# Layer 1's tail keys: future exponentials zeroed by GpSimd after the exponential, instead of a constant-mask matmul before it

## The chip, the cores and the metric

One Trainium2 chip, one of its cores. The metric is the device time of one execution in microseconds (us); the median of the runs is compared. The engines are TensorE (PE, with its weight loads as PEld), VectorE (DVE), ScalarE (ACT), GpSimd (POOL) and SyncE (SP), which issues most transfers.

## The reference, cut to what matters

Two layers of gated cross attention with a feed-forward part, on x of 4 batches x 512 rows x 128 channels; the keys and values come from a context of 154 rows per batch; 16 heads of 8 channels. What the change touches is layer 1's attention:

```python
scores = einsum('bhtd,bhsd->bhts', q, k) / sqrt(8)
causal = triu(full((512, 154), -inf), k=1)      # key s is seen by query t only if s <= t
attn = softmax(scores + causal, axis=-1)
out = einsum('bhts,bhsd->bhtd', attn, v)
x = x + tanh(g_xattn[1]) * (out @ Wo.T + bo)
```

Layer 0's attention has no causal mask. The feed-forward part of layer 1 is a recurrence over the 4 batches, with a gate of three matmul pairs for each.

## The kernel before, in words

Everything stays in SBUF. Each attention layer runs over the 4 batches as a software pipeline. For each batch there are 20 score tiles (index t, one per slot). Tiles 0 to 15 hold one head each: 128 keys on the partitions, 512 queries in a row. Keys 128 to 153 don't fit, so they are packed: tiles 16 to 19, the *tail tiles*, hold four heads each, in four blocks of 32 partitions; row r of a block is key 122 + r (TAIL0 is 122, OWN is 6, so rows 6 to 31 are the keys from 128 on). In layer 1 queries 0 to 127 see none of these keys, so a tail tile has only 384 queries.

For a tile, TensorE makes the scores in one of two PSUM banks (`scores`, L975 for the 16 main tiles, L981 for the tail tiles), ScalarE writes the exponential into the ring sb_pr of 8 tiles (`exps`, L766), and TensorE multiplies four tiles at a time with the values (`weigh`, L1007): rounds 0 to 3 take the main tiles, and two more calls, *tail0* and *tail1*, take the four tail tiles together. Both tail calls need the last exponential of the batch (tile 19). The sums go to two PSUM banks, which VectorE transposes and divides (L1332 to L1345); TensorE applies the output weights (L1016), VectorE adds the residual (L1351), and POOL and VectorE normalise.

Since only two score banks exist, the scores of tile k wait for the exponential of tile k - 2. The order of each engine's work is written out by hand: PE_PLAN, ACT_PLAN and DVE_PLAN give a slot (0 to 19) to each piece, and POOL's order is a loop over i. In iteration i the score tiles of batch i run, beside the tail calls of batch i - 1 (slots 1 and 3), the output product of batch i - 1 (slot 8), and the search for each query's largest score for batch i + 1 (L947, with its own mask L951, reduced by VectorE at L1312). Iteration i = 4 of layer 1 has no score tiles; there the tail calls of batch 3 come straight behind the last tile of iteration 3. The gate matmuls of the recurrence (`state` L1027 and `step` L1033, each run as two passes) are placed in the slots of iterations 3 and 4; `keep` and `renew` (L1366, L1373, L1376) update its state on VectorE.

The causal mask of layer 1 is made in two ways before the change. For the main tiles POOL zeroes the exponentials after ScalarE wrote them: `past(b, r)` (L614), one affine selection over four tiles, 128 partitions x 4 x 128, four times a batch; `weigh` waits for its semaphore past_r. For the tail tiles TensorE adds a constant of -2^126 to the scores before the exponential, with a second matmul of the identity by 32 columns of constants (L984, `maskE`), once for each tail tile:

```python
ins = pe.matmul(ps[:, q0:T], KT[:, b, t - H, :], Q4[n % 3][:, t - H, q0:T],
                start=True, stop=(layer == 0), skip_group_check=True)
if layer == 1:
    ins = pe.matmul(ps[:, P:P + 32], identr[:, :], maskE, start=False, stop=True, skip_group_check=True)
```

Only 32 of the 384 queries (128 to 159) can lie before one of these keys, so the mask has 32 columns.

POOL's loop in iteration i of layer 1: `past(i, 0)` to `past(i, 2)`, the normalisation of batch i - 1 (`normed`, L620 to L637), `past(i, 3)`, and `biased` for batch i + 1 (L598).

Of the kernel before, what the change touches and what calls it, by code (L numbers as in the profile page):

```python
# [8 lines left out]
F32R = mybir.dt.float32r  # L9
I16 = mybir.dt.int16  # L10
U16 = mybir.dt.uint16
ALU = mybir.AluOpType
# [3 lines left out]
P = 128  # L16
B, T, C = 4, 512, 128
TT = T // P
S = 154
H, D = 16, 8  # L20
G, J = 4, 4
NF = 3
TAIL0 = S - 32
OWN = P - TAIL0
SCALE = float(D) ** -0.5
EPS = 1e-5
NEG = -2.0 ** 126
# [9 lines left out]
TILES = H + G  # L37
# [3 lines left out]
PRING = 8  # L41
# [158 lines left out]
def program(nc, x, w, wkr, ctxT, tailT, wffn, cols, rows, consts, masks, out):  # L200
    with ExitStack() as ctx:  # L201
        def sb(name, shape, dt=F32):
            return ctx.enter_context(nc.sbuf_tensor("sb_" + name, shape, dt))

        def bank(name):
            return ctx.enter_context(nc.psum_tensor("ps_" + name, [P, 512], F32))

        def sem(name):
            return ctx.enter_context(nc.semaphore(name))
# [18 lines left out]
        ident = consts_sb[:, 0:P]  # L228
        own = consts_sb[:, P:P + 1]
        lowrow = consts_sb[:, P + 1:P + 2]  # L230
        cmask = sb("cmask", [P, 2 * P + 32])
        identr = sb("identr", [P, P], F32R)
        maskr = sb("maskr", [P, 2 * P + 32], F32R)
        maskM, maskT, maskE = maskr[:, 0:P], maskr[:, P:2 * P], maskr[:, 2 * P:2 * P + 32]
        ones = sb("ones", [P, P])
        onesr = sb("onesr", [2, P], F32R)
        bhl = sb("bhl", [2, 2, C], F32R)
# [26 lines left out]
        with ExitStack() as stretch:  # L264
            def sb_here(name, shape, dt=F32):
                return stretch.enter_context(nc.sbuf_tensor("sb_" + name, shape, dt))
# [16 lines left out]
            pr = sb_here("pr", [P, PRING, T])  # L283
# [27 lines left out]
        top = [bank(f"top{n}") for n in range(MRING)]  # L311
# [32 lines left out]
        nmh_r, nms_r, nmT_r = sem("nmh_r"), sem("nms_r"), sem("nmT_r")  # L344
        score_r, exp_r, pv_r = sem("score_r"), sem("exp_r"), sem("pv_r")
        pvx = sem("pvx")
        past_r = sem("past_r")
        oc_r, oT_r = sem("oc_r"), sem("oT_r")
        xg_r, res_r = sem("xg_r"), sem("res_r")
        wq_r, wT_r = sem("wq_r"), sem("wT_r")  # L350
# [111 lines left out]
        def _(pool):  # L462
# [125 lines left out]
            def biased(layer, b):  # L588
                n = B * layer + b
                if n >= 2:  # L590
                    pool.wait_ge(res_r, n - 1)
                if layer == 1:
                    pool.wait_ge(x2_r, b + 1)
                else:
                    pool.wait_ge(x_in[b], 16)
                pool.wait_ge(bias_r, 4)
                for t in range(TT):
                    ins = pool.tensor_tensor(xg[:, n % 2, t, :], xr[:, TT * b + t, :], bog[:, layer, :], ALU.add)  # L598
                ins.then_inc(xg_r, 1)
# [10 lines left out]
            def past(b, r):  # L610
# [3 lines left out]
                pool.affine_select(pr[:, k % PRING:k % PRING + 4, 0:P], pr[:, k % PRING:k % PRING + 4, 0:P],  # L614
                                   [[0, 4], [1, P]], ALU.is_ge, 0.0, base=0, channel_multiplier=-1).then_inc(past_r, 1)

            def root(k):

                pool.wait_ge(mv_r, k + 1)
                pool.tensor_scalar(var[:, k % 4, :], mv[:, k % 4, :, 1], EPS, 1.0, ALU.add, ALU.mult).then_inc(var_r, 1)  # L620
                pool.wait_ge(var_r, k + 1)
                pool.tensor_tensor(rstd[:, k % 4, :], var[:, k % 4, :], half[:, :], ALU.pow).then_inc(rstd_r, 1)  # L622
# [20 lines left out]
            for layer in range(2):  # L643
                normed("pre", layer, 0)
                if layer == 0:
                    pool.wait_ge(xn_r, 1)
                    pool.memset(Kd[1][:, :, :, :].bitcast(F32), 0.0).then_inc(kd_clear, 1)
                    pool.memset(V4[:, :, :, :, :], 0.0).then_inc(zero_r, 1)
                    pool.memset(VT[:, :, :, :], 0.0).then_inc(zero_r, 1)
                normed("pre", layer, 1)  # L650
                if layer == 0:
                    clear_rest()
                    normed("pre", 0, 2)
                    frames()
                    biases()
                    values(0)
                    q_low(0, 2)
                    tail_keys(0)
                else:
                    clear_late()  # L660
                for i in range(-1, B + 1):
                    masked = layer == 1 and 0 <= i < B
                    if i == -1 or 0 < i < B - 2:
                        b = max(i, 0) + 2
                        if i > 0:
                            normed("pre", layer, b)
                        if masked:
                            past(i, 0)
                        diagonal(layer, b)
                        if (layer, b) != (0, 2):  # L670
                            q_low(layer, b)
                    elif masked:
                        past(i, 0)
                    if masked:
                        past(i, 1)
                        past(i, 2)
                    if 0 <= i - 1 < B:
                        normed("post", layer, i - 1)
                    if masked:
                        past(i, 3)  # L680
                    if 0 <= i + 1 < B:
                        biased(layer, i + 1)
                if layer == 0:
                    pool.wait_ge(xq_r, B)
                    diagonal(1, 0)
                    values(1)
                    tail_keys(1)
                    clear_early()
# [205 lines left out]
        def _(pe):  # L894
# [70 lines left out]
            def scores(layer, b, t):  # L965
                n = B * layer + b
                k = TILES * n + t
                if t == 0:
                    pe.wait_ge(m_in[n % 3], 2 * 16 * (n // 3 + 1))
                if k >= SRING:  # L970
                    pe.wait_ge(exp_r, k - SRING + 1)
                ps = score[k % SRING]
                if t < H:
                    g, j = t % G, t // G
                    ins = pe.matmul(ps[:, :], Kd[n % 3][:, g, j, 0:P], Q4[n % 3][:, g, :], start=True,  # L975
                                    stop=True, skip_group_check=True)
                else:
                    if t == H and b == 0:
                        pe.wait_ge(kt_r, layer + 1)
                    q0 = P if layer == 1 else 0  # L980
                    ins = pe.matmul(ps[:, q0:T], KT[:, b, t - H, :], Q4[n % 3][:, t - H, q0:T],  # L981
                                    start=True, stop=(layer == 0), skip_group_check=True)
                    if layer == 1:
                        ins = pe.matmul(ps[:, P:P + 32], identr[:, :], maskE, start=False, stop=True,  # L984
                                        skip_group_check=True)
                ins.then_inc(score_r, 1)

            def weigh(layer, b, r):

                n = B * layer + b  # L990
                if r == 0 and b == 0:
                    pe.wait_ge(v_r, layer + 1)
                if (layer, r, b) == (1, 0, 0):
                    pe.wait_ge(x2_r, B)
                if r in (0, 2) and n > 0:
                    pe.wait_ge(pvx, 2 * (n - 1) + r // 2 + 1)
                if layer == 1 and r < 4:
                    pe.wait_ge(past_r, 4 * b + r + 1)
                pe.wait_ge(exp_r, TILES * n + (4 * r + 4 if r < 4 else TILES))
                acc = pv[r // 2 if r < 4 else r - 4]  # L1000
                q0 = P if layer == 1 and r >= 4 else 0
                for g in range(G):
                    if r < 4:
                        lhs, t = V4[:, b, g, r, :], 4 * r + g
                    else:
                        lhs, t = VT[:, b, g, 32 * (r - 4):32 * (r - 4) + 32], H + g
                    ins = pe.matmul(acc[32 * g:32 * g + 32, q0:T], lhs, pr[:, (TILES * n + t) % PRING, q0:T],  # L1007
                                    start=(r in (0, 2)), stop=(r >= 4), skip_group_check=True)
                ins.then_inc(pv_r, 1)
# [104 lines left out]
            for layer in range(2):  # L1114
# [44 lines left out]
                if layer == 0:  # L1159
# [8 lines left out]
                    for t in range(24):  # L1168
# [3 lines left out]
                        if t >= FRING:  # L1172
                            pe.wait_ge(fev, t - FRING + 1)
                        pe.matmul(fbank[t % FRING][:, :], wfT[:, 3 * (t // 12) + m, :], xq[:, c, :],
                                  start=True, stop=True).then_inc(fmm, 1)
# [20 lines left out]
            for t in range(TT):  # L1196
# [3 lines left out]
                          skip_group_check=True).then_inc(ymm, 1)  # L1200
# [401 lines left out]
def constants():  # L1602

    a = np.arange(P)
    ident = np.eye(P)
    top = np.where(a[None, :] > a[:, None], NEG, 0.0)
    main = np.where(a[:, None] > a[None, :], NEG, 0.0)
    tail = np.where((a % 32)[:, None] > np.arange(32)[None, :] + OWN, NEG, 0.0)
    own = (a % 32 >= OWN)[:, None]
    low = (a % PARTS == 2)[:, None]  # L1610
    return tuple(np.concatenate(parts, axis=1).astype(np.float32) for parts in ((ident, own, low), (top, main, tail)))


# [49 lines left out]
```

## Time and profile before

| what | value |
|---|---|
| median of 3 runs | 344.92 us (344.29 to 345.57) |
| the profiled execution's own time | 344.51 us |
| its span, first to last instruction | 342.5 us (2.0 us lie around it) |
| busy: PE, PEld, DVE, ACT, POOL | 280.7, 161.9, 252.1, 192.7, 136.4 us |
| instructions: PE, DVE, ACT, POOL | 1424, 538, 303, 274 |
| mean granted TensorE clock | 0.952 of full speed |

The busy times are sums over the span; whether an engine sets the end of a stretch is read from the chain of waits and from the timeline. Layer 1's score tiles run from about 228 to 314 us of the span.

### The profile page before, as it was taken

To read this page: it belongs to the slowest core of one execution; us is meant where nothing else is said; L and a number is where in the kernel's file an instruction comes from. 1 tells how busy PE (TensorE), PEld (TensorE's weight loads), DVE (VectorE), ACT (ScalarE), POOL (GpSimd) and SP (SyncE) were. 2 spreads that over 40 slices of the span, in tenths; PEclk is the share of its full clock that TensorE was granted. 3 is DMA by queue.
4 is the path that set the end of the run, shared out by engine and by line. 5 is a ranking of instruction groups with operands and counts; after the bars stand their busy time and mean duration, and the time that the engine had idled before them with its cause. 6 is when DMAs were issued, how large, how long until landed. Compare 5 with 4: busy or idle time off the path is not lost. (4 is left out here: it accounts for less than half of the span.)

```text
span 342.5 us, 4467 instructions
## 1 busy us (share of the span) xinstructions
PE 280.7 (82%) x1424; PEld 161.9 (47%) x1424; DVE 252.1 (74%) x538; ACT 192.7 (56%) x303; POOL 136.4 (40%) x274
## 2 busy tenths in 40 slices
PE   0889899899999878985007888899998998999994
PEld 0558544545433355331005776674554653443552
DVE  5699876978986287889989967985696693442833
ACT  1673366566466656779589632446556546664232
POOL 6669893750140411860002059911486107141100
PEclk9999999999999999996555999999999999999998
DMA  7840100110000000000000002220011000000004
GB/s 208 305 170 3 69 32 10 47 56 7 1 8 3 0 0 2 1 0 0 1 0 0 2 0 92 94 100 1 10 51 54 4 0 10 1 1 2 0 1 122
DMA packets 9687, 12.55 MB, mean 37 GB/s; under 512 B 896, under 2 KB 5376, under 8 KB 9664
## 3 DMA queue, kind: packets, MB, share of 16 engines
q1 hardware_dynamic: 9232, 11.80, 9.6%
q10 hardware_dynamic: 432, 0.47, 0.7%
q8 instruction: 11, 0.18, 0.2%
q14 instruction: 12, 0.10, 0.1%
HBM read 4.27 MB, written 1.05 MB: 16 GB/s over the span
## 5 line engine op out<-in xcount | busy, mean ns | idle before, releaser
L766 ACT ACTIVATE sb_pr<-ps_score 128x512 f32<-128x512 f32 (+1 forms) x160 | 89.0, 584 | 62.6 <-PE ps_score L975 52.4
L1312 DVE TENSOR_REDUCE sb_nm<-ps_top 128x3 f32<-128x462 f32 (+2 forms) x168 | 96.0, 626 | 26.6 <-PE ps_top L947 13.8
L947 PE MATMUL ps_top<-sb_Kd,sb_Q 128*128 128x462 f32 (+3 forms) x240 | 69.8, 350 | 4.7 <-DVE sb_nm L1312 2.4
L975 PE MATMUL ps_score<-sb_Q,sb_Kd 128*128 128x512 f32 x128 | 58.2, 469 | 1.8 <-ACT sb_pr L766 1.5
L947 PEld LDWEIGHTS ps_top<-sb_Kd,sb_Q 128*128 128x128 f32 x240 | 42.7, 189 | 18.1 <-DVE sb_nm L1312 11.9
L975 PEld LDWEIGHTS ps_score<-sb_Q,sb_Kd 128*128 128x128 f32 x128 | 23.7, 189 | 36.1 <-ACT sb_pr L766 27.9
L620 POOL TENSOR_SCALAR sb_var<-sb_mv 128x4 f32<-128x4 f32 x16 | 4.6, 290 | 83.7 <-DVE sb_mv L1275 83.2
L1007 PE MATMUL ps_pv<-sb_pr,sb_V 128*32 128x512 f32 x256 | 34.1, 605 | 0.0
L614 POOL TENSOR_SCALAR_AFFINE_SELECT sb_pr<-sb_pr 128x512 f32<-128x512 f32 x16 | 10.5, 658 | 46.5 <-ACT sb_pr L766 46.5
L1332 DVE STREAM_TRANSPOSE sb_oq<-ps_pv 128x512 f32<-128x512 f32 x16 | 10.8, 700 | 12.5 <-PE ps_pv L1007 12.3
L637 POOL TENSOR_SCALAR sb_xn<-sb_xr,sb_nmean,sb_rstd 128x128 f32<-128x128 f32 x44 | 19.1, 448 | 1.1
L622 POOL TENSOR_TENSOR sb_rstd<-sb_var,sb_half 128x4 f32<-128x4 f32 x16 | 17.7, 1105 | 1.3
L515 POOL CAST sb_Kd<-sb_K 32x616 fp32r<-32x616 f32 x20 | 14.0, 701 | 8.7 <-ACT sb_front L857 7.5
L981 PE MATMUL ps_score<-sb_Q,sb_KT 128*128 128x512 f32 (+1 forms) x32 | 14.3, 459 | 3.0 <-ACT sb_pr L766 3.0
L1085 PE MATMUL ps_top<-sb_wfT 128*128 128x256 f32 x30 | 9.9, 489 | 7.9 <-DVE sb_amax L1449 6.4
L1007 PE MATMUL ps_pv<-sb_pr,sb_VT 128*32 128x512 f32 (+1 forms) x128 | 14.9, 550 | 0.9 <-ACT sb_pr L766 0.9
L1272 DVE BATCH_NORM_STATS2 sb_stat<-sb_xr 128x6 f32<-128x128 f32 x64 | 13.9, 279 | 1.4 <-DMA sb_xr<-x 1.2
L491 POOL MEMSET sb_Q<- 128x2048 f32 x1 | 1.8, 1804 | 33.0 <-DVE sb_amax L1449 33.0
L924 PE MATMUL ps_misc<-sb_consts,sb_xn 128*128 128x128 f32 x64 | 10.6, 290 | 4.3 <-POOL sb_xn L637 1.6
L598 POOL TENSOR_TENSOR sb_xg<-sb_xr,sb_bog 128x128 f32<-128x128 f32 x32 | 13.6, 456 | 0.1
L1067 PE MATMUL ps_misc<-sb_consts,sb_amx 128*128 128x128 f32 x8 | 2.5, 401 | 13.2 <-DVE sb_amx L1382 13.2
L905 PE MATMUL ps_score<-sb_ctx,sb_wkr 128*128 128x308 f32 x16 | 6.1, 514 | 8.5 <-DMA sb_wkr<-wkr 8.5
(175 smaller groups left out, 549.9 us busy)
## 6 DMA issues: line engine op xcount, KB each, us to landing
sb_Q<-sb_qh SPq DMA_DIRECT2D x16, 256.0 KB, 2.3
sb_Q<-sb_ql SPq DMA_DIRECT2D x8, 256.0 KB, 3.2
sb_xr<-x SPq DMA_DIRECT2D x4, 256.0 KB, 8.0
out<-sb_xr SPq DMA_DIRECT2D x4, 256.0 KB, 2.5
sb_wsb<-w SPq DMA_DIRECT2D x1, 704.0 KB, 8.4
sb_wf<-wffn SPq DMA_DIRECT2D x1, 576.0 KB, 8.5
sb_wkr<-wkr SPq DMA_DIRECT2D x2, 256.0 KB, 7.0
sb_Q<-sb_nmT SPq DMA_DIRECT2D x16, 32.0 KB
```

The lines of the kernel that those rows point to most:

```text
L515: ins = pool.tensor_copy(Kd[n % 3][q, :, j, :], K4[q, :, b, :])
L598: ins = pool.tensor_tensor(xg[:, n % 2, t, :], xr[:, TT * b + t, :], bog[:, layer, :], ALU.add)
L622: pool.tensor_tensor(rstd[:, k % 4, :], var[:, k % 4, :], half[:, :], ALU.pow).then_inc(rstd_r, 1)
L637: ins = pool.tensor_scalar(xn[:, kind == "post", t, :], xr[:, TT * b + t, :], nmean[:, k % 4, t:t + 1], rstd[:, k % 4, t:t + 1], ALU.add, ...
L766: act.activation(pr[:, k % PRING, q0:T], score[k % SRING][:, q0:T], ACT.Exp, scale=SCALE).then_inc(exp_r, 1)
L947: ins = pe.matmul(cols[:, c0:c1, :], Q4[n % 3][:, g, P * qt:P * qt + P], Kd[n % 3][:, g, j:j + c1 - c0, 0:keys], start=True, stop=not mask ...
L975: ins = pe.matmul(ps[:, :], Kd[n % 3][:, g, j, 0:P], Q4[n % 3][:, g, :], start=True, stop=True, skip_group_check=True)
L981: ins = pe.matmul(ps[:, q0:T], KT[:, b, t - H, :], Q4[n % 3][:, t - H, q0:T], start=True, stop=(layer == 0), skip_group_check=True)
L1007: ins = pe.matmul(acc[32 * g:32 * g + 32, q0:T], lhs, pr[:, (TILES * n + t) % PRING, q0:T], start=(r in (0, 2)), stop=(r >= 4), skip_group ...
L1272: ins = dve.bn_stats(stat6[:, k % 4, t, :], xr[:, TT * b + t, :])
L1312: dve.tensor_reduce(nm[:, :, :].rearrange("p t h -> p (t h)")[:, f0:f0 + heads], top[k % MRING][:, 0:keys * heads].rearrange("p (h k) -> p ...
L1332: dve.transpose(oq[:, part, :, :, :].rearrange("p k e r -> p (k e r)"), pv[part][:, :]).then_inc(pvx, 1)
```

## The change

`tail_past(b)` is new: after the last exponential of batch b (and after POOL's own `biased` of that iteration) POOL zeroes the future exponentials in place, with four affine selections, one for each block of 32 partitions, each over 4 tiles x 32 queries. Each waits for the one before it on POOL's own chain of semaphores, and POOL waits for the last before it goes on. Both tail calls of `weigh` now also wait for it. The 16 mask matmuls of the tail tiles and their constants are gone. `scores_for_top` keeps its own mask. The core of the diff:

```diff
-        cmask = sb("cmask", [P, 2 * P + 32])
+        cmask = sb("cmask", [P, 2 * P])
-        maskr = sb("maskr", [P, 2 * P + 32], F32R)
-        maskM, maskT, maskE = maskr[:, 0:P], maskr[:, P:2 * P], maskr[:, 2 * P:2 * P + 32]
+        maskr = sb("maskr", [P, 2 * P], F32R)
+        maskM = maskr[:, 0:P]
...
+            def tail_past(b):
+
+                k = TILES * (B + b) + H
+                pool.wait_ge(exp_r, k + G)
+                for j in range(J):
+                    own_tail = pr[32 * j:32 * j + 32, k % PRING:k % PRING + G, P:P + 32]
+                    ins = pool.affine_select(own_tail, own_tail, [[0, G], [1, 32]], ALU.is_ge, 0.0, base=OWN,
+                                             channel_multiplier=-1)
+                    if j < J - 1:
+                        link(ins)
+                ins.then_inc(tail_past_r, 1)
+                pool.wait_ge(tail_past_r, b + 1)
...
                     if 0 <= i + 1 < B:
                         biased(layer, i + 1)
+                    if masked:
+                        pool.wait_ge(xg_r, min(B + i + 2, 2 * B))
+                        tail_past(i)
...
                     ins = pe.matmul(ps[:, q0:T], KT[:, b, t - H, :], Q4[n % 3][:, t - H, q0:T],
-                                    start=True, stop=(layer == 0), skip_group_check=True)
-                    if layer == 1:
-                        ins = pe.matmul(ps[:, P:P + 32], identr[:, :], maskE, start=False, stop=True,
-                                        skip_group_check=True)
+                                    start=True, stop=True, skip_group_check=True)
...
-                if layer == 1 and r < 4:
-                    pe.wait_ge(past_r, 4 * b + r + 1)
+                if layer == 1:
+                    pe.wait_ge(*((past_r, 4 * b + r + 1) if r < 4 else (tail_past_r, b + 1)))
```

Where it moves instructions. POOL, from iteration 0 of layer 1 into iteration 1 (sb_pr is the ring of exponentials, sb_xg the residual with its bias, sb_var and sb_rstd the normalisation). Before:

```order
L598 TENSOR_TENSOR sb_xg<-sb_xr,sb_bog 128x128 [waits bias_r,x2_r,res_r]
L598 TENSOR_TENSOR sb_xg<-sb_xr,sb_bog 128x128 x3
L620 TENSOR_SCALAR sb_var<-sb_mv 128x4 [waits mv_r]
L622 TENSOR_TENSOR sb_rstd<-sb_var,sb_half 128x4 [waits var_r]
L630 TENSOR_SCALAR sb_nmean<-sb_mv 128x4
```

And now:

```order
L598 TENSOR_TENSOR sb_xg<-sb_xr,sb_bog 128x128 [waits bias_r,x2_r,res_r]
L598 TENSOR_TENSOR sb_xg<-sb_xr,sb_bog 128x128 x3
L623 AFFINE_SELECT sb_pr<-sb_pr 32x4x32 [waits exp_r,xg_r]
L623 AFFINE_SELECT sb_pr<-sb_pr 32x4x32 [waits pool_chain] x3
L633 TENSOR_SCALAR sb_var<-sb_mv 128x4 [waits mv_r,tail_past_r]
L635 TENSOR_TENSOR sb_rstd<-sb_var,sb_half 128x4 [waits var_r]
```

Four selections stand between the bias and the next normalisation; they wait for the batch's last exponential, and the normalisation now also waits for them.

TensorE, from the last tail tile of batch 2 into batch 3 (L975 and L991 are the scores of main tiles, L1007 and L1020 `weigh`). Before:

```order
L981 MATMUL ps_score<-sb_Q,sb_KT 128x384 [waits exp_r]
L984 MATMUL ps_score<-sb_maskr,sb_identr 128x32
L975 MATMUL ps_score<-sb_Q,sb_Kd 128x512 [waits exp_r,m_in1]
L975 MATMUL ps_score<-sb_Q,sb_Kd 128x512 [waits exp_r]
L1007 MATMUL ps_pv<-sb_pr,sb_VT 32x384 [waits exp_r]
L1007 MATMUL ps_pv<-sb_pr,sb_VT 32x384 x3
L975 MATMUL ps_score<-sb_Q,sb_Kd 128x512 [waits exp_r] x2
L1007 MATMUL ps_pv<-sb_pr,sb_VT 32x384 [waits exp_r]
```

And now:

```order
L997 MATMUL ps_score<-sb_Q,sb_KT 128x384 [waits exp_r]
L991 MATMUL ps_score<-sb_Q,sb_Kd 128x512 [waits exp_r,m_in1]
L991 MATMUL ps_score<-sb_Q,sb_Kd 128x512 [waits exp_r]
L1020 MATMUL ps_pv<-sb_pr,sb_VT 32x384 [waits exp_r,tail_past_r]
L1020 MATMUL ps_pv<-sb_pr,sb_VT 32x384 x3
L991 MATMUL ps_score<-sb_Q,sb_Kd 128x512 [waits exp_r] x2
L1020 MATMUL ps_pv<-sb_pr,sb_VT 32x384 [waits exp_r,tail_past_r]
```

The mask matmul behind the tail tile is gone, nothing else changes its place, and the tail call waits for POOL as well as for ScalarE.

## Rows read from the trace of the kernel before

**Rows 1.** The page, part 1: busy time, share of the span, instructions.

```profile
PE 280.7 (82%) x1424; PEld 161.9 (47%) x1424; DVE 252.1 (74%) x538; ACT 192.7 (56%) x303; POOL 136.4 (40%) x274
```

**Rows 2.** Busy time of each engine by stretch, layer 1 (windows view).

```profile
core 0: us, PE busy (x) PEld busy (x) DVE busy (x) ACT busy (x) POOL busy (x), PEclk, DMA share, GB/s
...
290.00:303.00 13.00, 12.74 (x63) 5.44 (x62) 6.04 (x16) 7.56 (x15) 1.27 (x2) 1.00 0.00 1
303.00:317.00 14.00, 12.93 (x66) 5.58 (x63) 3.65 (x6) 8.06 (x15) 4.54 (x9) 1.00 0.01 2
```

**Rows 3.** The chain that ended last, in order of time: start us, us, what.

```profile
289.81 0.50 ACT sb_pr L766
...
290.85 0.78 PE ps_pv L1007 x8
291.63 0.66 PE ps_score L975 x2
...
295.23 0.46 PE ps_score L975 x2
...
316.13 0.70 DVE sb_cst L1376
...
316.87 1.13 PE ps_top L1027 x2
```

**Rows 4.** The mask matmuls' weight loads (line L984): duration ns min/median/max.

```profile
L984 PEld LDWEIGHTS ps_score<-sb_maskr,sb_identr x16: 187/190/191, 239.5 to 313.3; 128*128 128x128 f32 x16
```

**Rows 5.** Timeline, around the mask matmul of batch 3's tile 18.

```profile
309.74 0.19 PEld L984 LDWEIGHTS ps_score<-sb_maskr,sb_identr 128*128 128x128 f32 x1 [0.24 <-issue]
...
309.92 0.42 PEld L924 LDWEIGHTS ps_misc<-sb_consts,sb_xn 128*128 128x128 f32 x4
```

**Rows 6.** Timeline, last exponentials (tile 19) and tail0 of batches 0, 1, 3.

```profile
243.81 0.49 ACT L766 ACTIVATE sb_pr<-ps_score 128x384 f32<-128x384 f32 x1 [1.46 <-PE ps_score L984]
...
245.45 0.16 PEld L1007 LDWEIGHTS ps_pv<-sb_pr,sb_VT 128*32 128x32 f32 x8
...
250.54 0.66 PE L924 MATMUL ps_misc<-sb_consts,sb_xn 128*128 128x128 f32 x4 [0.24 <-POOL sb_xn L637]
...
267.76 0.49 ACT L766 ACTIVATE sb_pr<-ps_score 128x384 f32<-128x384 f32 x1 [0.79 <-PE ps_score L984]
...
269.41 0.16 PEld L1007 LDWEIGHTS ps_pv<-sb_pr,sb_VT 128*32 128x32 f32 x8 [0.16 <-issue]
...
290.78 0.16 PEld L1007 LDWEIGHTS ps_pv<-sb_pr,sb_VT 128*32 128x32 f32 x8 [0.25 <-ACT sb_pr L766]
...
313.73 0.49 ACT L766 ACTIVATE sb_pr<-ps_score 128x384 f32<-128x384 f32 x1 [0.36 <-PE ps_score L984]
...
314.57 1.50 PE L1007 MATMUL ps_pv<-sb_pr,sb_VT 128*32 128x384 f32 x16
```

**Rows 7.** POOL by line: duration ns min/median/max; then one stretch, and one group.

```profile
L614 POOL TENSOR_SCALAR_AFFINE_SELECT sb_pr<-sb_pr x16: 634/635/827, 230.1 to 308.5; 128x512 f32<-128x512 f32 x16
L528 POOL CAST sb_KT<-sb_K x8: 599/610/1229, 43.8 to 151.4; 32x512 fp32r<-32x512 f32 x8
L515 POOL CAST sb_Kd<-sb_K x20: 687/694/776, 46.5 to 253.4; 32x616 fp32r<-32x616 f32 x20
L579 POOL TENSOR_TENSOR sb_VT<-sb_tmp,sb_bvt x32: 239/243/1022, 37.4 to 147.1; 32x32 f32<-32x32 f32 x32
...
37.43 5.07 POOL L579 TENSOR_TENSOR sb_VT<-sb_tmp,sb_bvt 32x32 f32<-32x32 f32 x16
...
L560 POOL TENSOR_SCALAR sb_VT<-sb_ones,sb_consts 32x128 f32<-32x128 f32 x4 | 1.5, 366 | 0.4
```

**Rows 8.** Timeline, POOL's normalisation ahead of TensorE's start at 250.54.

```profile
248.75 1.73 POOL L637 TENSOR_SCALAR sb_xn<-sb_xr,sb_nmean,sb_rstd 128x128 f32<-128x128 f32 x4
```

**Rows 9.** Timeline, one of POOL's selections beside VectorE.

```profile
275.78 0.76 DVE L1338 TENSOR_TENSOR sb_oc<-sb_oq,sb_orc 128x256 f32<-128x256 f32 x2
...
276.21 0.83 POOL L614 TENSOR_SCALAR_AFFINE_SELECT sb_pr<-sb_pr 128x512 f32<-128x512 f32 x1 [3.47 <-ACT sb_pr L766]
```

More of the change, by code:

```diff
@@ L346, in program @@
         pvx = sem("pvx")
-        past_r = sem("past_r")
+        past_r, tail_past_r = sem("past_r"), sem("tail_past_r")
         oc_r, oT_r = sem("oc_r"), sem("oT_r")
@@ L1607, in constants @@
     main = np.where(a[:, None] > a[None, :], NEG, 0.0)
-    tail = np.where((a % 32)[:, None] > np.arange(32)[None, :] + OWN, NEG, 0.0)
     own = (a % 32 >= OWN)[:, None]
     low = (a % PARTS == 2)[:, None]
-    return tuple(np.concatenate(parts, axis=1).astype(np.float32) for parts in ((ident, own, low), (top, main, tail)))
+    return tuple(np.concatenate(parts, axis=1).astype(np.float32) for parts in ((ident, own, low), (top, main)))
 def kernel(**inputs):
```

## The prediction

> **What bounds the kernel now.** I read the page's busy times, the windows of layer 1, the chain of waits, and then the timeline at the four places where a batch's last exponential is followed by its tail calls. The page says little by itself: TensorE is busy 82% of the span [rows 1], an average over unlike stretches. The windows say more: from 290 to 303 us TensorE is busy 12.74 of 13.00 us, from 303 to 317 us 12.93 of 14.00, at the full granted clock, and POOL only 1.27 and 4.54 us [rows 2]. So in layer 1 a matmul less is worth time, and POOL has idle time to take work. But the question is not how much POOL can do; it is when. The mask has been made *before* the exponential, by an engine that runs ahead; now it is made *after* it, between the exponential and the matmul that needs it. The timeline tells how much room there is [rows 6]: the last exponential of batch 0 ends at 243.81 + 0.49 = 244.30 and tail0 starts at 245.45, 1.15 us later; batch 1: 268.25 and 269.41, 1.16; batch 2: 290.31 [rows 3] and 290.78, 0.47; batch 3: 314.22 and 314.57, 0.35. At batch 2 the chain runs straight from that exponential into the tail call [rows 3].
>
> **What the removal is worth.** A mask matmul streams only 32 columns, but needs the whole identity as its weights: 16 loads of 190 ns [rows 4]. Where TensorE is the bound, the next weight load starts 309.92 - 309.74 = 0.18 us after the mask's [rows 5]; I take 0.18 us for each mask. Not all of the 16 count. The timeline shows tile 17's scores waiting for ScalarE in batches 0 to 2 (tile 18's too in batch 2), so a mask ahead of that wait was free. That leaves 3, 3 and 1 masks before the tail calls of batches 0, 1 and 2 (0.54, 0.54, 0.18 us), of which the last comes after the batch's last scores for batches 0 and 1: the last exponential itself comes 0.36, 0.36 and 0.18 us earlier. In batch 3 all four count, less 0.06 because tile 17 then meets its wait: 0.66, and 0.48 ahead of the last exponential.
>
> The Trainium skill, page "TensorE: Matmul & The Clock Gate", section "LDWEIGHTS (loading the stationary operand)", gives a weight load as its columns divided by 1.2, so 107 ns for 128 columns, where the rows have 190. By it a mask would be worth 0.11 us, the last exponentials would come 0.14, 0.14, 0.07 and 0.21 us later than I take them, and the sum would be 0.56 us higher; the measured load decides.
>
> **What the selections cost.** The trace has no selection over 32 partitions x 4 x 32. The nearest is POOL's own over 128 x 4 x 128: 635 ns for 512 elements a partition [rows 7]. Two POOL casts give the price of an element: 610 ns at 512 and 694 at 616, 0.81 ns each [rows 7]. Taking 384 elements off: 635 - 384 x 0.81 = 324 ns; both patterns have four rows, so no cost by row is left out. That the number of partitions doesn't matter I read from the casts, which have 32 and lie beside the selection, which has 128. I take 0.32 us. Bounds: below, the shortest POOL instruction on 32 partitions that reads and writes, 0.243 us for 32 elements; above, 0.366 us, a two-step POOL operation on 32 x 128; far above, 0.635 us, if elements cost nothing [all rows 7]. The link between chained ones: 16 took 5.07 us, so (5.07 - 0.24) / 15 - 0.24 = 0.08 us [rows 7]. Four selections and three links: 4 x 0.32 + 3 x 0.08 = 1.52 us. A hand-over takes 0.06 us (POOL's normalisation ends at 248.75 + 1.73 = 250.48 [rows 8], TensorE starts at 250.54 [rows 6]); I take as much from ScalarE to POOL. So tail0 can start **1.64 us** after the last exponential (bounds 1.33 and 1.82; 2.90 far above). The wait on POOL's own bias costs nothing: in all iterations that work ends before the exponential.
>
> **Place by place** (tail0's start, then what reaches the end):
> - Batch 0: 244.30 - 0.36 + 1.64 = 245.58 against 245.45: 0.13 late. TensorE comes there 0.54 early and waits. Behind it, at 250.54, TensorE idled 0.24 us for POOL's normalisation [rows 6]; that chain (VectorE's reductions, statistics, POOL) does not pass the tail call, gets the 0.5 us, and POOL has finished its selections before VectorE's statistics arrive. So 0.13 - 0.24 = **-0.11**.
> - Batch 1: 268.25 - 0.36 + 1.64 = 269.53 against 269.41: **+0.12**. TensorE is continuous behind it until VectorE's reductions, which wait for it.
> - Batch 2: 290.31 - 0.18 + 1.64 = 291.77 against 290.78: 0.99. Of it, 0.20 comes back: the two score tiles behind tail0 took 0.66 us since the second waited for ScalarE, and take 0.46 when ScalarE is ahead [rows 3]. **+0.79**, with TensorE the bound for 10 us after.
> - Batch 3: the last exponential ends at 314.22 - 0.48 = 313.74; selections until 315.38. Here VectorE updates the state with two-input instructions from some 314.7 us on. A selection beside one took 0.83 us instead of 0.635 [rows 9], 30% more; half of the four overlap, +0.15. The two tail calls take 1.50 us [rows 6]: 315.53 + 1.50 = 317.03. Behind them is the gate matmul that now starts at 316.87, right when VectorE's state is ready (316.13 + 0.70 [rows 3]). That path comes 0.66 earlier, so the tails decide: **+0.16**.
>
> The 32 columns of constants less in ScalarE's copy are worth 32 x 0.81 ns, -0.03 at most, by POOL's price for lack of a nearer one. Nothing queued behind POOL's new wait is due before it ends: the next selection needs exponentials of the next batch. Sum: -0.11 + 0.12 + 0.79 + 0.16 - 0.03 = **+0.93 us**. Of the profiled execution's 344.51 us this makes 345.4; the median of the runs lies 0.41 higher, so I forecast **345.8 us**: 2.3 us of TensorE work bought back with waits. With the bounds of a selection (0.31 shorter, 0.18 longer at each of four places): -0.3 and +1.65, so 344.6 to 346.6. A measurement of this kernel can tell about 0.5%, 1.7 us, from no change.
>
> **The rivals.**
> 1. *POOL's fixed cost rules.* Place: the four tail calls; price: at 0.635 us a selection each tail call is 1.26 us later, 4 x 1.26 + 0.93 = +6.0, 350.9 us. For it: software on POOL need not scale. Against it: the casts do. Slower than 0.5% begins at 0.37 us a selection (0.20 us more at each place). Chance 0.09.
> 2. *VectorE is beside POOL at all four places.* Price: 30% on 1.28 us, +0.38, at batches 0 to 2, and 0.23 more at batch 3: +2.3, 347.2 us. Against it: at batches 0 and 1 the timeline has VectorE reducing from PSUM and taking one-input statistics, at batch 2 idle. The Trainium skill, "GPSIMD Engine Reference", section "Specifications", says that POOL's way into SBUF is shared with VectorE and contended by VectorE's two-port modes and its instructions with two SBUF inputs; the row agrees for two inputs. Chance 0.07.
> 3. *The mask matmuls freed nothing*, since the next weight load waits anyway for something else. Then the last exponentials stay: +0.25, +0.48, +0.97, +0.64, less 0.03: +2.3, 347.2 us. Against it: rows 5. Chance 0.06.
> 4. *The selections are hidden* and all masks pay: -0.54 - 0.54 - 0.18 - 0.66, 343.0 us. For batches 0 and 1 this needs 0.99 us instead of 1.64, so 0.16 us a selection, below every reading and writing POOL row; for batch 2 it needs still less. Chance 0.08.
>
> **How the numbers follow.** The forecast keeps 0.70. Its range with the bounds is 344.6 to 346.6; the runs of before spread 0.6 us about their median, which takes the lower end to 343.9, and rivals 2 and 3 the upper to 347.3. Left out are rivals 4 and 1, 0.17. Faster by over 0.5%: rival 4, 0.08. Slower: rivals 1 to 3, 0.22. Within: 0.70.
>
> **What would show it.** Right: 4 x 4 = 16 selections of 32 partitions at about 0.32 us, 16 mask matmuls gone; TensorE idle before tail0 with POOL as its releaser, some 0.6 us for batches 0 and 1, over 1 us for batch 2, the largest; last exponentials earlier against the work before them. Wrong: selections at 0.37 us or more; no idle before tail0; or the tail calls of batch 3 no longer setting the start of the gate matmul behind them.

## The result and the profile after

| | kernel before | the change |
|---|---|---|
| median of all runs | 344.88 us (344.29 to 345.57, 5 runs) | 346.26 us (346.19 to 347.55, 5 runs) |
| ratio to before, 95% interval | | 1.0054 (1.0041 to 1.0067) |
| the profiled execution's own time | 344.51 us | 346.24 us |
| its span | 342.5 us | 344.3 us |

The change makes the kernel slower by half a per cent. The forecast of 345.8 us lies 0.46 us below the median of the runs, the measured time is inside the range, and the ratio's interval straddles the 0.5% that divides "within" from "slower". As a cost it is 1.38 us between the medians (0.54%, or 1.86 us, by the ratio), where +0.93 was forecast. The first line of the page after, to hold against [rows 1]:

```profile
PE 277.8 (81%) x1408; PEld 159.2 (46%) x1408; DVE 252.0 (73%) x538; ACT 192.7 (56%) x303; POOL 141.5 (41%) x290
```

TensorE has 16 instructions and 2.9 us less to do, and the span is 1.8 us longer. Where the work went shows in the windows of the change (the same columns and stretches as [rows 2]):

```profile
290.00:303.00 13.00, 11.90 (x54) 5.46 (x55) 5.12 (x12) 6.67 (x12) 2.47 (x6) 1.00 0.00 1
303.00:317.00 14.00, 12.24 (x51) 4.72 (x49) 3.69 (x10) 9.07 (x16) 6.02 (x13) 1.00 0.00 0
```

TensorE, busy 12.74 and 12.93 us there before, now has gaps, at the same full granted clock. What fills them is in the chain of waits of the change, where [rows 3] had one exponential, one score matmul (290.35, 0.50 us, L975; the prediction's "straight" passes over it) and then the tail call (start us, us, what):

```profile
289.98 0.50 ACT sb_pr L782
290.60 0.31 POOL sb_pr L623
290.96 0.31 POOL sb_pr L623
291.33 0.31 POOL sb_pr L623
291.70 0.32 POOL sb_pr L623
292.06 0.85 PE ps_pv L1020 x8
292.92 0.66 PE ps_score L991 x2
...
314.69 0.50 ACT sb_pr L782
315.31 0.31 POOL sb_pr L623
315.68 0.31 POOL sb_pr L623
316.04 0.31 POOL sb_pr L623
316.41 0.73 POOL sb_pr L623
317.19 1.50 PE ps_pv L1020 x16
318.69 1.05 PE ps_top L1040 x2
```

All four places are on the chain with their four selections in series: batches 2 and 3 as shown, batch 0 from 244.49 and batch 1 from 268.18 us. The timeline of the change has the same at each place ([rows 6] before; the bracket is TensorE's idle time and who ended it):

```profile
245.95 0.85 PE L1020 MATMUL ps_pv<-sb_pr,sb_VT 128*32 128x384 f32 x8 [0.49 <-POOL sb_pr L623]
...
269.65 0.85 PE L1020 MATMUL ps_pv<-sb_pr,sb_VT 128*32 128x384 f32 x8 [0.49 <-POOL sb_pr L623]
...
292.06 0.85 PE L1020 MATMUL ps_pv<-sb_pr,sb_VT 128*32 128x384 f32 x8 [1.05 <-POOL sb_pr L623]
...
317.19 1.50 PE L1020 MATMUL ps_pv<-sb_pr,sb_VT 128*32 128x384 f32 x16 [1.67 <-POOL sb_pr L623]
```

0.49, 0.49, 1.05 and 1.67 us of idle time, each released by POOL. The selections by line, and the four of batch 3 with VectorE beside them:

```profile
L623 POOL TENSOR_SCALAR_AFFINE_SELECT sb_pr<-sb_pr x16: 298/300/721, 244.5 to 316.4; 32x128 f32<-32x128 f32 x16
...
315.31 1.82 POOL L623 TENSOR_SCALAR_AFFINE_SELECT sb_pr<-sb_pr 32x128 f32<-32x128 f32 x4 [4.86 <-ACT sb_pr L782]
...
316.27 0.69 DVE L1386 SCALAR_TENSOR_TENSOR sb_tmp<-sb_gt 128x512 f32<-128x512 f32 x1 [4.72 <-ACT sb_gt L791]
317.00 0.69 DVE L1389 SCALAR_TENSOR_TENSOR sb_cst<-sb_tmp 128x512 f32<-128x512 f32 x1
```

A selection takes 300 ns and starts 0.37 us after the one before; the last of batch 3, beside VectorE's update of the state, takes 721 ns.

**A clock that starts at the change.** The trace of the change lies 0.28 us later than that of before already when layer 1's tail work begins, and 0.25 of that by 18 us (a copy of ScalarE's starts at 18.37 and 18.62), ahead of every changed instruction but the transfer of the constants. So I measure from one matmul of batch 0 of layer 1 (L961 before, L977 now: the transposed maxima, at 238.85 and 239.13) to the gate matmul behind the last tail calls (316.87 and 318.62): 78.02 and 79.49 us, **+1.47**. Together with the 0.28 this is the 1.75 us by which the gate matmul came later. By places (batch 0: from this matmul to the same one of batch 1; batch 1: from there to that of batch 2; batch 2: on to tail0; batch 3: from tail0 of batch 2 to the gate matmul), all against before. The matmuls of before (290.78 is in [rows 6]):

```profile
238.85 0.61 PE L961 MATMUL ps_misc<-sb_consts,sb_nms 128*32 128x128 f32 x4
...
262.36 0.61 PE L961 MATMUL ps_misc<-sb_consts,sb_nms 128*32 128x128 f32 x4 [0.26 <-DVE sb_nms L1325]
...
285.30 0.61 PE L961 MATMUL ps_misc<-sb_consts,sb_nms 128*32 128x128 f32 x4 [0.21 <-DVE sb_nms L1325]
...
316.87 1.13 PE L1027 MATMUL ps_top<-sb_cst,sb_wsb 128*128 128x512 f32 x2 [0.80 <-DVE sb_cst L1376]
```

and of the change (292.06 is above):

```profile
239.13 0.61 PE L977 MATMUL ps_misc<-sb_consts,sb_nms 128*32 128x128 f32 x4
...
262.38 0.61 PE L977 MATMUL ps_misc<-sb_consts,sb_nms 128*32 128x128 f32 x4 [0.25 <-DVE sb_nms L1338]
...
285.55 0.61 PE L977 MATMUL ps_misc<-sb_consts,sb_nms 128*32 128x128 f32 x4 [0.25 <-DVE sb_nms L1338]
...
318.62 1.12 PE L1040 MATMUL ps_top<-sb_cst,sb_wsb 128*128 128x512 f32 x2
```

| kernel | batch 0 | batch 1 | batch 2 | batch 3 | sum |
|---|---|---|---|---|---|
| the change | -0.26 | +0.23 | +1.03 | +0.47 | +1.47 |
| neither mask nor selection (below) | -0.35 | -0.36 | -0.09 | -0.40 | -1.20 |
| both (below) | +0.09 | +0.43 | +1.10 | +0.88 | +2.50 |
| one multiplication (below) | -0.28 | -0.35 | +0.08 | -0.38 | -0.93 |

Each row is one profiled execution. How far they can be trusted shows in the first try of "VectorE waits" below, whose added wait does nothing: its places are -0.27, +0.23, +1.03 and +0.46, sum +1.45, within 0.02 us of the change's.

### The profile page after: what moved, and what is told of

Its sections match the earlier page's. It is cut to its first block and busy times, and to the rows that moved or that the text cites. A ratio compares the mean times of both kernels' runs of the same rounds, so it can differ in the third digit from the quotient of the medians.

```text
span 344.3 us, 4467 instructions
## 1 busy us (share of the span) xinstructions
PE 277.8 (81%) x1408; PEld 159.2 (46%) x1408; DVE 252.0 (73%) x538; ACT 192.7 (56%) x303; POOL 141.5 (41%) x290
## 3 DMA queue, kind: packets, MB, share of 16 engines
HBM read 4.26 MB, written 1.05 MB: 15 GB/s over the span
## 5 line engine op out<-in xcount | busy, mean ns | idle before, releaser
L991 PE MATMUL ps_score<-sb_Q,sb_Kd 128*128 128x512 f32 x128 | 58.1, 468 | 1.6 <-ACT sb_pr L782 1.2
L991 PEld LDWEIGHTS ps_score<-sb_Q,sb_Kd 128*128 128x128 f32 x128 | 23.6, 188 | 36.2 <-ACT sb_pr L782 25.8
L1020 PE MATMUL ps_pv<-sb_pr,sb_V 128*32 128x512 f32 x256 | 34.1, 605 | 0.0
L1020 PE MATMUL ps_pv<-sb_pr,sb_VT 128*32 128x512 f32 (+1 forms) x128 | 14.9, 550 | 4.6 <-POOL sb_pr L623 3.7
L1098 PE MATMUL ps_top<-sb_wfT 128*128 128x256 f32 x30 | 9.0, 453 | 8.8 <-DVE sb_amax L1462 6.4
```

## The experiments

Each edit is against the kernel with the change.

**Neither, and both.** Two kernels that take the change apart into what it removes and what it adds. The first leaves out the selections and their wait; in it layer 1's tail keys are not masked at all, so that part of the causal mask is left out.

```diff
-                    if masked:
-                        pool.wait_ge(xg_r, min(B + i + 2, 2 * B))
-                        tail_past(i)
...
-                if layer == 1:
-                    pe.wait_ge(*((past_r, 4 * b + r + 1) if r < 4 else (tail_past_r, b + 1)))
+                if layer == 1 and r < 4:
+                    pe.wait_ge(past_r, 4 * b + r + 1)
```

> Neither the mask matmuls nor the selections (layer 1's tail keys then see the future: that part of the mask is left out). Theory 1 (the change loses by a serial hold between the last exponential and the tail call, and wins back what the mask matmuls cost on TensorE): in the trace of the change TensorE reaches the tail calls some 0.11 us earlier per mask, not 0.18, so 344.9 - (0.3 + 0.3 + 0.1 + 0.4) = 343.8 us, no wait on POOL before a tail call. Theory 2 (the mask matmuls freed nothing, weight loads bound anyway): 344.9 us, the same as before.

The second keeps the selections and puts the mask matmuls and their constants back.

```diff
-                                    start=True, stop=True, skip_group_check=True)
+                                    start=True, stop=not (layer == 1), skip_group_check=True)
+                    if layer == 1:
+                        ins = pe.matmul(ps[:, P:P + 32], identr[:, :], maskE, start=False, stop=True,
+                                        skip_group_check=True)
```

> Mask matmuls kept and the selections done as well. Theory 1: the hold at its full price, the last exponentials come as late as before: 346.3 + 0.23 + 0.22 + 0.08 + 0.32 = 347.1 us. Theory 2: 346.3 us, as the change.

Measured: neither 343.46 us, ratio 0.9959 (0.9945 to 0.9974); both 347.33 us, 1.0077 (1.0058 to 1.0096). Both lie nearer to what a hold at four places predicts than to the other theory. The sums of the table make a square of four kernels: the 16 masks are worth 1.20 us without the selections (before less neither) and 2.50 - 1.47 = 1.03 us with them; the hold costs 2.50 us with the masks in place, and 1.47 + 1.20 = 2.67 us without. So the price of the hold (2.34 by rival 3's sum) was close, and the gain was sized too high: 1.92 us expected when all masks pay (rival 4's sum), 1.20 found.

**Without the links.** Each selection signals by itself; TensorE and POOL wait for the fourth.

```diff
-                    if j < J - 1:
-                        link(ins)
-                ins.then_inc(tail_past_r, 1)
-                pool.wait_ge(tail_past_r, b + 1)
+                    ins.then_inc(tail_past_r, 1)
+                pool.wait_ge(tail_past_r, J * (b + 1))
...
-                    pe.wait_ge(*((past_r, 4 * b + r + 1) if r < 4 else (tail_past_r, b + 1)))
+                    pe.wait_ge(*((past_r, 4 * b + r + 1) if r < 4 else (tail_past_r, J * (b + 1))))
```

> The four selections of a batch without the links between them (they touch different partitions); TensorE waits for all four. Theory 1a (four selections run one after the other, only the links of 0.07 us go): 1.41 becomes 1.2 us, 345.5 us. Theory 1b (POOL overlaps instructions on different partitions): 1.41 us falls to 0.6 or less, and the time to 344.2 us. Theory 2 (the hold is not what costs): 346.3 us.

Measured: 346.23 us, 1.0043 (1.0027 to 1.0059). Theories 1a and 1b both missed. The time is the one that theory 2 named (346.3), but it does not speak for that theory: the edit did not shorten the hold, so it does not test what the hold costs. The chain of waits of this kernel, batch 0:

```profile
244.64 0.30 POOL sb_pr L623
245.00 0.30 POOL sb_pr L623
245.37 0.30 POOL sb_pr L623
245.73 0.32 POOL sb_pr L623
```

The start-to-start time stays 0.36 to 0.37 us, four selections 1.41 us (244.64 to 245.73 + 0.32 = 246.05), as with the links. The 0.07 us between one selection and the next is not the wait's; and four selections over four different sets of partitions run one after another all the same.

**One multiplication.** If the price of the hold is a number of POOL instructions in series, one instruction over all 128 partitions should do: the 32 columns of each tile times a constant pattern of zeros and ones.

```diff
+                if b == 0:
+                    pool.wait_ge(mask_in, 16)
...
-                for j in range(J):
-                    own_tail = pr[32 * j:32 * j + 32, k % PRING:k % PRING + G, P:P + 32]
-                    ins = pool.affine_select(own_tail, own_tail, [[0, G], [1, 32]], ALU.is_ge, 0.0, base=OWN,
-                                             channel_multiplier=-1)
-                    if j < J - 1:
-                        link(ins)
-                ins.then_inc(tail_past_r, 1)
+                own_tail = pr[:, k % PRING:k % PRING + G, P:P + 32]
+                pool.tensor_tensor(own_tail, own_tail, cmask[:, 2 * P:2 * P + 32].unsqueeze(1).to_broadcast([P, G, 32]),
+                                   ALU.mult).then_inc(tail_past_r, 1)
...
+    keep = np.where((a % 32)[:, None] > np.arange(32)[None, :] + OWN, 0.0, 1.0)
```

> The four selections replaced by one POOL multiplication over 128 partitions x 4 x 32 with constant zeros and ones. From the 128 x 128 two-input POOL rows: 0.46 us, so a hold of 0.65 us instead of 1.6. Theory 1: batch 2 still some 0.3 us late, the rest as without any mask: 344.1 us. Theory 2: 346.3 us.

Measured: **344.02 us** (343.66 to 344.89), ratio 0.9976 (0.9966 to 0.9986). It is faster than both kernels. Its timeline at batch 2:

```profile
291.03 0.46 POOL L624 TENSOR_TENSOR sb_pr<-sb_pr,sb_cmask 128x128 f32<-128x128 f32 x1 [0.96 <-ACT sb_pr L780]
291.54 0.16 PEld L1018 LDWEIGHTS ps_pv<-sb_pr,sb_VT 128*32 128x32 f32 x8 [0.42 <-POOL sb_pr L624]
```

0.46 us stand where 1.41 stood. In batches 0 and 1 this fits into the 1.15 us of room that [rows 6] show (the table has them within 0.07 us of the kernel with no mask at all); in batch 3 the gate matmul waits for VectorE's state again, not for the tails. Only batch 2 pays, 0.17 us more than with no mask. The run changes the operation along with the number of instructions; one selection over 128 partitions x 4 x 32 was not run. One caution, by arithmetic and not from a run: a selection writes zero whatever it finds, a multiplication of an infinite exponential by zero does not, so this version relies on future exponentials staying finite.

**Selections where there is room.** Selections in batches 0 and 1, masks in batches 2 and 3.

```diff
-                    if masked:
+                    if masked and i < 2:
...
+                    if layer == 1 and b >= 2:
+                        ins = pe.matmul(ps[:, P:P + 32], identr[:, :], maskE, start=False, stop=True,
+                                        skip_group_check=True)
...
-                if layer == 1:
+                if layer == 1 and (r < 4 or b < 2):
```

> Selections for batches 0 and 1, mask matmuls for batches 2 and 3. Theory 1 (each place pays its own hold; measured between the same rows of the traces, the change loses -0.26, +0.23, +1.03 and +0.47 us at batches 0 to 3): batches 2 and 3 fall back to nothing, so 0.0 us in all, 344.8 us, no different from before. Rival (the loss is not tied to places, half the selections cost half): 345.5 us.

Measured: 344.85 us against 344.99 of before beside it, 1.0001 (0.9988 to 1.0013). Measured from the same matmul it is 0.07 us shorter than before, by places -0.28, +0.22, 0.00 and -0.01. So the loss of the change as a whole is all in batches 2 and 3, where the tail call had 0.47 and 0.35 us of room. In the first two the selections gain at one batch about what they lose at the other.

**One wait less.** POOL no longer waits for its own bias ahead of the selections.

```diff
-                        pool.wait_ge(xg_r, min(B + i + 2, 2 * B))
```

> The change without POOL's wait on its own bias ahead of the selections. The traces show 0.13 us from the last exponential to the first selection, against 0.05 us for the selections of the main tiles, which have one wait. If the second wait is the cause: 0.05 us here, tail calls of batches 1 to 3 each 0.08 us earlier, 346.0 us. If not: 0.13 us and 346.3 us.

Measured: 346.13 us, 1.0043 (1.0029 to 1.0058): not to be told from the change. The hand-over can be read, though. Timeline of this kernel at batch 0:

```profile
243.82 0.49 ACT L781 ACTIVATE sb_pr<-ps_score 128x384 f32<-128x384 f32 x1 [1.35 <-PE ps_score L996]
244.38 1.41 POOL L623 TENSOR_SCALAR_AFFINE_SELECT sb_pr<-sb_pr 32x128 f32<-32x128 f32 x4 [1.21 <-ACT sb_pr L781]
```

From the exponential's end (244.31) to POOL 0.07 us, as at the other three places; with the wait it was 0.14 (243.86 + 0.49 = 244.35 to 244.49 in the change; 0.12 to 0.13 at the other three places). A wait that has long been fulfilled still cost some 0.06 us, where the prediction put it at nothing.

**VectorE waits.** If VectorE's update slows the last selection of batch 3, then an update that waits for the selections should leave all 16 at one length. The first try had the wait at the wrong batch's update:

```diff
+                if b == 2:
+                    dve.wait_ge(tail_past_r, B)
```

> VectorE's update of the state for batch 2 waits until POOL's last selections are done. Theory (two-input VectorE instructions slow the POOL selection beside them): the last selection of batch 3 falls from 0.72 to 0.30 us, tail0 of batch 3 comes 0.4 us earlier, and the gate matmul behind it too, as its state is ready at about the time the tails end: 345.9 us. Rival (the last selection is slow whatever VectorE does): 0.72 us still, and the update only comes later: 346.3 us or more.

Measured: 346.03 us, 1.0037 (1.0023 to 1.0050), with the last selection still at 721 ns. The update beside the selections is the recurrence's step for its batch 1, so the wait was idle, and this run says nothing on the question; it is a repeat of the change, as used under the table. The second try:

```diff
+                if b == 1:
+                    dve.wait_ge(tail_past_r, B)
```

> As the run before it, but with the wait where it belongs: the update that runs beside batch 3's selections is batch 1's step of the recurrence, not batch 2's. Theory (two-input VectorE instructions slow the POOL selection beside them): the last selection falls from 0.72 to 0.30 us, tail0 of batch 3 starts 0.4 us earlier; the update now starts behind the selections, so the gate matmul gains some 0.3 us: 345.9 us. Rival (the last selection is slow whatever VectorE does): still 0.72 us, the gate matmul waits for the later update: 346.6 us.

Measured: 345.62 us, 1.0022 (1.0010 to 1.0033). By line, and in the timeline of batch 3:

```profile
L623 POOL TENSOR_SCALAR_AFFINE_SELECT sb_pr<-sb_pr x16: 299/302/308, 245.5 to 317.5; 32x128 f32<-32x128 f32 x16
...
316.37 1.41 POOL L623 TENSOR_SCALAR_AFFINE_SELECT sb_pr<-sb_pr 32x128 f32<-32x128 f32 x4 [4.84 <-ACT sb_pr L782]
...
317.81 0.69 DVE L1388 SCALAR_TENSOR_TENSOR sb_tmp<-sb_gt 128x512 f32<-128x512 f32 x1 [5.20 <-POOL sb_pr L623]
```

All 16 selections now take 0.30 us, and the four of batch 3 take 1.41 instead of 1.82; the stretch to the gate matmul is 79.11 us instead of 79.49. So the slow selection came from VectorE's instruction beside it, and delaying VectorE by that much costs next to nothing here: its state is ready at 318.54 + 0.69 = 319.23, and the tails' recorded end is 317.83 + 1.50 = 319.33.

## Why the prediction was right, and where its terms were off

**The mechanism held.** A serial hold of POOL behind the last exponential, at four places, that eats up the time of the masks: the chain of waits shows it, the square of four kernels prices it, and the two versions that shorten it (one multiplication) or leave it out of the tight batches (split) take the loss away. The hold itself came out as predicted at batches 0 to 2: 245.95 - 244.35 = 1.60 us at batch 0, and 292.06 - (289.98 + 0.50) = 1.58 at batch 2, against 1.64. In its parts it did not: the selections were cheaper (0.30 us, and 1.41 for four against 1.52), the hand-over from ScalarE dearer (0.13 against 0.06, by the second wait), which nearly cancels. That batch 2 has the largest cost held too (+1.03); but the longest idle time before tail0, which the prediction also put there, was batch 3's, 1.67 us against 1.05. Of it, 0.80 us only took the place of a wait that stood behind the tail calls before, ahead of the gate matmul (316.87 above). The claim on batch 3 that the tail calls would come to set the gate matmul's start held (VectorE's state is ready at 317.00 + 0.69 = 317.69, the tails end at 318.69).

**The step that failed: a mask's worth.** I took 0.18 us, the time from the mask's weight load to the next load [rows 5]. Batch 0's second tail tile (tile 17) shows what was wrong. The kernel before:

```profile
240.61 0.45 PE L981 MATMUL ps_score<-sb_Q,sb_KT 128*128 128x384 f32 x1 [0.73 <-ACT sb_pr L766]
...
240.72 0.19 PEld L984 LDWEIGHTS ps_score<-sb_maskr,sb_identr 128*128 128x128 f32 x1
...
240.90 0.19 PEld L947 LDWEIGHTS ps_top<-sb_Kd,sb_Q 128*128 128x128 f32 x1
240.92 0.48 PE L947 MATMUL ps_top<-sb_Kd,sb_Q 128*128 128x512 f32 x1
...
241.47 0.34 PE L981 MATMUL ps_score<-sb_Q,sb_KT 128*128 128x384 f32 x1
```

and the change:

```profile
240.90 0.44 PE L997 MATMUL ps_score<-sb_Q,sb_KT 128*128 128x384 f32 x1 [0.76 <-ACT sb_pr L782]
...
241.00 0.19 PEld L963 LDWEIGHTS ps_top<-sb_Kd,sb_Q 128*128 128x128 f32 x1
241.18 0.40 PE L963 MATMUL ps_top<-sb_Kd,sb_Q 128*128 128x512 f32 x1
...
241.65 0.34 PE L997 MATMUL ps_score<-sb_Q,sb_KT 128*128 128x384 f32 x1
```

Counted from the tail tile's scores, the next load starts at 0.10 instead of 0.29, earlier by 0.19; but the matmul behind it ends at 0.68 instead of 0.79, and the next tail tile starts at 0.75 instead of 0.86: 0.11 earlier. The load that came free sooner brings its own matmul forward by little: that starts 0.28 us after the scores' start instead of 0.31 (241.18 - 240.90 and 240.92 - 240.61). What holds it there no row says. A gap between two loads is not a gap between two results; the step should have been counted from one matmul of the same kind to the next. Over 16 masks the worth was 1.20 us (0.35, 0.36, 0.09 and 0.40 by places, where 0.54, 0.54, 0.18 and 0.66 were taken). That is 0.075 for each of the 16, or 0.11 for each of the 11 that the prediction let count: which masks pay was about right, what one pays was not. The last exponentials came 0.23, 0.22, 0.08 and 0.32 us earlier (each against the clock of its own place) instead of 0.36, 0.36, 0.18 and 0.48. In batch 3 some of the masks freed less still: tile 18's was worth 0.06 us up to the next value product (310.51 - 309.34 = 1.17 before, 311.50 - 310.39 = 1.11 now).

The 0.11 us is also what an estimate from the Trainium skill's page "TensorE: Matmul & The Clock Gate", section "LDWEIGHTS (loading the stationary operand)", gave for a mask (107 ns, its figure for a load of 128 columns). The trace does not bear out that figure for the load, which is recorded with 187 to 191 ns [rows 4]; it is the net worth that came to this size, and no run shows that the one follows from the other.

**The recovery that did not come.** I counted on 0.20 us back at batch 2, since the two score tiles behind tail0 took 0.66 us "since the second waited for ScalarE". In the change ScalarE is done at 291.68, well ahead, and they take 0.66 us again (292.92 in the chain above; [rows 3] before). So that was no wait for ScalarE, but part of the time of two matmuls behind a tail call: there the first weight load starts only 0.07 us before the call's recorded end (292.84 against 292.06 + 0.85).

**Contention was in the right place with the wrong size.** At batch 3 I took 30% on half of the selections, 0.15 us, from one row of a larger selection [rows 9]; 30% of half of 1.28 us is 0.19. It was one selection with 0.42 us more, and the run in which VectorE waits shows the cause. The Trainium skill, "GPSIMD Engine Reference", section "Specifications", says that VectorE's instructions with two SBUF inputs contend with POOL; the trace agrees, 721 against 302 ns.

**The sum.** Predicted for the four places was +0.96, measured +1.47. The 0.51 us between them: the tail calls of batches 0 and 2 came 0.09 and 0.04 later than predicted, and batch 1's place took 0.11 more; 0.24 more than predicted came back behind tail0 of batch 0 (below); 0.20 is the recovery; 0.16 is batch 3's masks (0.48 less 0.32); 0.22 is batch 3's hold (2.01 us from 315.18 to 317.19, against 1.79); and 0.07 is that the gate matmul begins that much before the recorded end of the tails. 0.09 + 0.11 + 0.04 - 0.24 + 0.20 + 0.16 + 0.22 - 0.07 = 0.51. So in the first two batches the errors nearly cancelled, which is luck, and batches 2 and 3 carry what is left. That the inner bounds, 344.6 to 346.6, held the result is partly luck too: they were built from the price of a selection, which came out 0.02 us from what was taken. A mask's worth, the largest of the errors (0.13, 0.14, 0.10 and 0.16 us at the four last exponentials), had room only in the outer end of the range, by rival 3.

The 0.24 us of batch 0 is mostly a misreading of an idle time. Before, TensorE's 0.24 us of idle time ahead of 250.54 [rows 6] were taken for all that could come back. The matmul ahead of it:

```profile
249.91 0.39 PE L947 MATMUL ps_top<-sb_Kd,sb_Q 128*128 128x308 f32 x1
```

and the same two in the change, where POOL no longer holds the second:

```profile
250.41 0.39 PE L963 MATMUL ps_top<-sb_Kd,sb_Q 128*128 128x308 f32 x1
250.63 0.60 PE L940 MATMUL ps_misc<-sb_consts,sb_xn 128*128 128x128 f32 x4
```

From start to start it is 0.63 us before and 0.22 now, so 0.41 came back here and not 0.24. Another 0.07 came back between there and batch 1, and why is open. Idle time, too, is better read from one matmul's start to the next one's.

The rivals: none took place. Rival 1's fixed cost is out (a selection of 32 partitions takes 0.30, not 0.635 us), rival 2's contention is there at one place of four, rival 3 is half right in that a mask freed less than its load's time, and rival 4, which needed 0.16 us a selection, is what the one multiplication comes near to in its waits (0.46 us for all four), though not in its time (344.0, not 343.0), since the masks are worth 1.20 and not 1.92 us. By the prediction's own rows the hold that rival 4 needs at batch 0 is 1.15 + 0.36 - 0.54 = 0.97 us, not 0.99; this changes nothing.

What else stays open is what the 0.28 us ahead of layer 1's tail work are. In the other traces the same difference runs from -0.13 (split) to 1.33 us (the second try of "VectorE waits"), and the profiled execution of the kernel with one multiplication has 1.31; it was the slowest of its 12 runs, 344.89 us, and yet its stretch from there is 0.93 us shorter than before.

## What to carry to other kernels

Work that is moved from before an exponential to after it is priced by the room between producer and consumer at each place, not by the idle share of the engine that gets it: here 1.15, 1.16, 0.47 and 0.35 us of room against a hold of 1.6 (2.0 at the last place). Such a hold is a number of instructions in series, so here one multiplication over all partitions (0.46 us) beat four selections over a quarter each (1.41). And the worth of a matmul removed is read from one matmul to the next of the same kind, not from the spacing of weight loads.

## What was not expected of the hardware

- On POOL, selections over separate blocks of 32 partitions followed each other at 0.37 us with or without semaphores between them.
- A second wait, long fulfilled, made the hand-over from ScalarE to POOL 0.13 instead of 0.07 us.
- One two-input instruction on VectorE stretched a selection of 32 x 128 from 0.30 to 0.72 us, by more than the larger one in [rows 9] was (0.635 to 0.83).
